# CIN tower of a DLRM: embedding columns by way of a DRAM scratch, and a tile's last partial sums on VectorE

## What is computed

```python
B, F0, D = (256, 39, 16)      # F0 = 39 fields, D = 16; the batch here is 1024
x0 = inputs; xk = inputs; outs = []
for W in filters:             # f0 (39*39, 128), f1 (128*39, 128), f2 (128*39, 128)
    b, f, d = x0.shape
    g = xk.shape[1]
    z = jnp.einsum('bfd,bgd->bfgd', x0, xk).reshape(b, f * g, d)
    cur = jnp.einsum('bpd,pm->bmd', z, W)
    outs.append(cur)
    xk = cur
result = jnp.sum(jnp.concatenate(outs, axis=1), axis=-1)
...
e = jnp.stack([tbl_0[ids[:, 0]], ..., tbl_38[ids[:, 38]]], axis=1)
```

## Time and profile before

| | |
|---|---|
| median of 3 runs | 1393.21 us (1392.9 to 1393.88) |
| profiled execution | 1393.13 us, of which the span of the instructions 1391.3 us |
| mean granted clock of TensorE | 0.998 |
| busy: TensorE, its weight loads | 93%, 70% |
| busy: VectorE, ScalarE, GpSimd | 70%, 55%, 75% |
| VectorE's MACs (L805) | 2944, 811.6 us |
| ScalarE's scaling (L667) | 2048, 585.8 us |
| GpSimd's adds (L364, L368) | 565.0 and 58.8 us |
| gathers (L341) | 312, 298.9 us |
| DMA | 72.97 MB, mean 52 GB/s |

### The profile page before, as it was taken

The page is one execution under the profiler, slowest core; times in us unless marked ns, Lnnn a source line. Parts: engine busy times, 40 slices in busy tenths (PEclk is TensorE's granted clock), DMA queues, the critical chain, the costliest instruction groups (busy, mean ns, idle before and its releaser), DMA issues.

```text
span 1391.3 us, 25265 instructions
## 1 busy us (share of the span) xinstructions
PE 1294.6 (93%) x5629; PEld 971.1 (70%) x5629; DVE 978.5 (70%) x3241; ACT 760.4 (55%) x2434; POOL 1038.3 (75%) x921
## 2 busy tenths in 40 slices
PE   0179999998999999999999999999999999999999
PEld 0057777776778777877778767877778777877754
DVE  2068778687876878688876778687885878688720
ACT  2136565466655566466664566466664565566631
POOL 7648868788787878788787878878787876566530
PEclk9999999999999999999999999999999999999999
DMA  8131122011211112111211112111211111111000
GB/s 220 25 112 53 47 70 64 6 54 46 80 53 52 47 38 74 27 53 47 79 53 52 47 24 64 50 53 47 78 53 53 46 25 58 51 52 45 1 1 0
DMA packets 73417, 72.97 MB, mean 52 GB/s; under 512 B 32428, under 2 KB 44690, under 8 KB 72716
## 3 DMA queue, kind: packets, MB, share of 16 engines
q1 hardware_dynamic: 60600, 67.88, 16.5%
q0 software_dynamic: 9984, 2.58, 2.2%
q10 hardware_dynamic: 2720, 1.48, 0.4%
HBM read 10.15 MB, written 0.00 MB: 7 GB/s over the span
## 4 chain that ended last, share of the span: by engine, by line
PE 50%; POOL 14%; DVE 11%; issue 10%; DMA 6%; ACT 5%; SPq 3%; DVEq 1%; POOLq 0%; ACTq 0%
PE ps L469 10%; PE ps L473 10%; PE ps L470 10%; PE ps L448 9%; DVE terms L805 9%; POOL terms L364 6%; POOL x_in L341 5%; PE ps L493 5%; DMA x_cols<-x_cols 4%; ACT terms L667 3%; DVE prods L777 3%; PE ps L558 2%; PE ps L483 2%; POOL prods_low L218 2%; DMA x_first<-x_cols 1%
## 5 line engine op out<-in xcount | busy, mean ns | idle before, releaser
L805 DVE SCALAR_TENSOR_TENSOR terms<-ps,x_scal,terms 128x128 f32<-128x128 f32 x2944 | 811.6, 346 | 276.0 <-PE ps L473 149.3
L667 ACT ACTIVATE terms<-ps,x_scal 128x128 f32<-128x128 f32 x2048 | 585.8, 375 | 388.6 <-PE ps L473 342.1
L364 POOL TENSOR_TENSOR terms<-terms 128x1024 f32<-128x1024 f32 (+2 forms) x384 | 565.0, 1471 | 168.2 <-DVE terms L805 142.9
L469 PE MATMUL ps<-w_high,x_high 128*128 128x512 f32 (+1 forms) x1280 | 592.5, 463 | 24.3 <-DVE terms L805 18.6
L473 PE MATMUL ps<-w_high,x_low 128*128 128x512 f32 (+1 forms) x1280 | 499.7, 390 | 6.1 <-ACT x_cols L619 5.6
L470 PE MATMUL ps<-w_low,x_high 128*128 128x512 f32 (+1 forms) x1280 | 497.8, 389 | 0.0
L341 POOL DMA_INDIRECT x_in<-in_tbl,ids_now x312 | 298.9, 958 | 100.5 <-issue 84.6
L469 PEld LDWEIGHTS ps<-w_high,x_high 128*128 128x128 f32 x1280 | 241.4, 189 | 136.5 <-DVE terms L805 50.5
L470 PEld LDWEIGHTS ps<-w_low,x_high 128*128 128x128 f32 x1280 | 242.4, 189 | 71.0 <-issue 29.8
L473 PEld LDWEIGHTS ps<-w_high,x_low 128*128 128x128 f32 x1280 | 241.2, 188 | 60.2 <-ACT x_cols L619 8.2
L448 PE MATMUL ps<-prods,w 117*128 117x512 f32 x262 | 135.3, 601 | 8.6 <-DVE prods L777 8.6
(11 more groups left out here) (45 smaller groups left out, 455.0 us busy)
## 6 DMA issues: line engine op xcount, KB each, us to landing
prods<-x_cols SPq DMA_DIRECT2D x192, 234.0 KB
x_first<-x_cols SPq DMA_DIRECT2D x96, 78.0 KB
x_in<-in_tbl,ids_now POOLq DMA_INDIRECT x312
x_cols<-x_cols SPq DMA_DIRECT2D x14, 312.0 KB
x_diag<-x_scal SPq DMA_DIRECT2D x256, 9.8 KB, 1.9
s<-in_f SPq DMA_DIRECT2D x3, 832.0 KB, 13.2
wt<-in_W_top ACTq DMA_DIRECT2D x1, 768.0 KB, 8.0
wt<-in_W_top ACTq DMA_DIRECT2D x1, 512.0 KB, 9.3
```

What stands on the lines that cost most here:

```text
L364: nc.gpsimd.tensor_tensor(t[:, 0:n], t[:, 0:n], t[:, n:2 * n], ALU.add).then_inc(s_tree, 1)
L469: nc.tensor.matmul(y, x1_high[:, par, at:at + P], high, start=True, stop=False)
L667: op = nc.scalar.activation(terms[:, u % 2, FB * ACT_BANKS.index(q) + i, :], ps[:, (BANKS * u + q) % RING, i * G:(i + 1) * G], ACT.Copy, s ...
L805: nc.vector.scalar_tensor_tensor(out=acc, in0=y, scalar=x0, in1=acc, op0=ALU.mult, op1=ALU.add).then_inc(s_mac, 1)
```

## The change

x0 is fetched by groups of 32 samples and no longer by batches. On the host, the 39 tables are joined into one, and the ids are ordered so that one indirect DMA fetches four fields of 32 samples; GpSimd adds the tables' first rows to the ids (`number_rows`). Ten gathers make a group. A DMA (`put`) writes the group to a scratch in DRAM, `rows`, and four DMAs (`load_cols`) read it back into x0_cols with the fields on partitions, the repeats included. The transposes, `store_cols` and `repeat` go. Gathers run three groups ahead (`AHEAD`). SP's queue is ordered anew (`feed`); w2 and the MLP's weights are loaded later, behind the first x_diag, from SP's queue, and TensorE waits for w2 after the second tile. GpSimd's tree ends at four slices (`TREE = (8, 4)`), and VectorE sums these four into x2 (`reduce`), for tile u - 1 behind bank 9 of tile u, ahead of a product that stands there. The diff, cut to its core:

```diff
-GATHERED, SUMMED = 8, 10
-TURNS = ((9, 7), (10, 0), (10, 4), (10, 8))
-TREE = (8, 4, 2)
+SAMPLES = P // GROUPS
+FOUR = P // SAMPLES
+FETCHES = -(-F // FOUR)
+AHEAD = 3
+TREE = (8, 4)
+LEFT = TREE[-1]
+REDUCE_AT = 9
...
+        def put(queue, bt, j):
+
+            queue.wait_ge(s_gather[j % 2], (bt * (GROUPS // 2) + j // 2 + 1) * (16 * FETCHES))
+            queue.dma_start(rows[j % GROUPS].rearrange("(n p) d -> p n d", p=P), x0_in[:, j % 2, :, :]).then_inc(s_put, 16)
+
+        def load_cols(queue, gf, j):
+
+            g = j % GROUPS
+            queue.wait_ge(s_put, gf * 16 + 16)
+            source = rows[g].rearrange("(f b) d -> f (b d)", b=SAMPLES)
+            for i in range(SPT + 1):
+                n = min(F, CYCLIC - i * F)
+                queue.dma_start(x0_cols[i * F:i * F + n, g * GCOLS:(g + 1) * GCOLS], source[0:n, :]).then_inc(s_load, 16)
...
+            def next_cols(gf, j):
+
+                sp.wait_ge(s_load, gf * (16 * (SPT + 1)) + 16 * (SPT + 1))
+                move_first(j)
+
+            def feed(bt, j, more=True):
+
+                gf = bt * GROUPS + j
+                move(gf, j)
+                if more:
+                    put(sp, bt, j + 1)
+                move_diag(gf, j)
+                if more:
+                    load_cols(sp, gf + 1, j + 1)
+                    next_cols(gf + 1, j + 1)
 
             load_ids(1)
-            sp.wait_ge(s_cols, 1)
-            repeat(slice(0, GCOLS), 1)
+            put(sp, 0, 0)
+            load_cols(sp, 0, 0)
+            next_cols(0, 0)
             move(0, 0)
+            next_cols(1, 1)
+            move(1, 1)
             sp.wait_ge(s_ones, 1)
             sp.wait_ge(s_scal, 1)
             for b in range(TB):
...
+            load_late()
+            put(sp, 0, 2)
+            move_diag(1, 1)
+            load_cols(sp, 2, 2)
+            next_cols(2, 2)
+            for j in range(2, GROUPS + 1):
+                feed(0, j)
+            with sp.Fori(1, NBATCH - 1) as bt:
+                load_ids(bt + 1)
+                for j in range(1, GROUPS + 1):
+                    feed(bt, j)
...
                     nc.gpsimd.tensor_tensor(t[:, 0:n], t[:, 0:n], t[:, n:2 * n], ALU.add).then_inc(s_tree, 1)
-                pool.wait_ge(s_tree, bt * (STEPS * len(TREE)) + len(TREE) * (u + 1))
-
-                pool.wait_ge(s_s3, bt * STEPS + u - 1 + CREDIT_S3)
-                nc.gpsimd.tensor_tensor(x2[:, u % 2], t[:, 0], t[:, 1], ALU.add).then_inc(s_x2, 1)
...
+            with pool.Fori(0, NBATCH - 1) as bt:
+                for u in range(STEPS):
+                    if u == TILES:
+                        pool.wait_ge(s_ids, bt * 16 + 3 * 16)
+                        pool.wait_ge(s_gather[1], (bt * (GROUPS // 2) + GROUPS // 2) * (16 * FETCHES))
+                        number_rows()
+                        pool.wait_ge(s_row, bt + 2)
+                    if u % TILES == 0:
+                        pool.wait_ge(s_put, (bt * GROUPS + u // TILES + AHEAD - 1) * 16)
+                    add_up(bt, u)
+                    for n in gathers(u):
+                        gather(u // TILES + AHEAD, n)
...
-                if turn_next:
-                    may_turn(bt, TURNS.index((u, q)))
+                if scalars_next:
+                    pe.wait_ge(s_load, (bt * GROUPS + u // TILES + 2) * (16 * (SPT + 1)))
...
+                    if u == 1 and q == BANKS - 1:
+                        pe.wait_ge(s_w2, 16)
...
-                store_first_cols(slice(0, GCOLS // D), 1)
                 store_scalars(0, 0, False)
-                store_first_cols(slice(GCOLS // D, BATCH), 3)
                 store_first(0, 0, FIRST_BANK)
+                act.wait_ge(s_put, 16)
+                act.wait_ge(s_load, 16 * (SPT + 1))
+                put(act, 0, 1)
+                load_cols(act, 1, 1)
                 store_x1(0, 0)
...
+            def reduce(bt, u):
+
+                dve.wait_ge(s_tree, bt * (STEPS * len(TREE)) + len(TREE) * (u + 1))
+                dve.wait_ge(s_s3, bt * STEPS + u - 1 + CREDIT_S3)
+                nc.vector.tensor_reduce(x2[:, u % 2], terms[:, u % 2, 0:LEFT, :].rearrange("p t g -> p g t"),
+                                        AX_X, ALU.add).then_inc(s_x2, 1)
...
                     if q in DVE_BANKS:
                         mac(bt, u, q)
+                    if q == REDUCE_AT and u > 0:
+                        reduce(bt, u - 1)
                     if front and (tile, q) in PRODUCTS:
                         multiply(bt, j, PRODUCTS.index((tile, q)), X1_BANK)
```

More of the change, by code:

```diff
@@ L161, in cin_tower @@
         s_top = sem("mlp_weights_loaded")
-        s_gather = sem("rows_gathered")
+        s_dense = sem("dense_loaded")
+        s_gather = [sem(f"rows_gathered{i}") for i in range(2)]
         s_ones = sem("x0_diag_cleared")
@@ L311, in _ @@
             for b in range(TB):
[L312 to L328, removed]
+                rows_b = slice(b * D, (b + 1) * D)
+                sp.dma_start(x0_diag[rows_b, 0, :, b, 0:F], x0_scal[rows_b, 0, :, :]).then_inc(s_diag[0], 16)
+            load_late()
[9 more added lines that the diff above has]
+                    feed(bt, j)
+            for j in range(1, GROUPS):
+                feed(NBATCH - 1, j, j < GROUPS - 1)
             for h in range(2):
@@ L401, in _ @@
+            for u in range(STEPS):
+                if u == 0:
+                    pool.wait_ge(s_put, (NBATCH * GROUPS - 2) * 16)
+                add_up(NBATCH - 1, u, u < STEPS - TILES)
+                if u < TILES:
+                    for n in gathers(u):
+                        gather(u // TILES + AHEAD, n)
         @block.tensor
@@ L507, in prologue @@
                 pe.wait_ge(s_dene, NBATCH // 4)
-                pe.wait_ge(s_gather, 16 * F)
-                for r in range(4):
-                    turn(r, r)
-                pe.wait_ge(s_cols, 1)
+                pe.wait_ge(s_load, 16 * (SPT + 1))
                 turn_scalars(0, 0)
@@ L527, in step @@
                 for q in range(BANKS):
-                    turns = not last and (u, q) in TURNS
+                    scalars = front and (tile, q) == SCALARS
                     if (tile, q) == SCALARS and j == 2:
                         pe.wait_ge(s_r, bt * 2 + CREDIT_R)
-                    cin2(bt, u, q, turns)
+                    cin2(bt, u, q, scalars)
                     if q == S3_AT and u >= 2:
                         sum_s3(bt, u)
-                    if turns:
-                        turn(TURNS.index((u, q)), MISC_BANK)
-                    if front and (tile, q) == SCALARS:
+                    if scalars:
                         turn_scalars(gf, j)
@@ L722, in step @@
                         store_s3(bt, u)
-                    if not last and (u, q) in TURNS:
-                        store_cols(bt + 1, TURNS.index((u, q)))
                     if front and (tile, q) == SCALARS:
@@ L844, in step @@
                         split_x1(gf, j)
[L846 removed]
+            prologue_then_batches(dve, step, prologue, lambda bt: reduce(bt, STEPS - 1))
 TOP = ("W_top1", "b_top1", "W_top2", "b_top2", "W_top3")
@@ L878 @@
     out = nc.dram_tensor("out_y", (B, 1), F32, kind="ExternalOutput").ap()
-    cin_tower(nc, ap["dense_ctx"], ap["ids"], [ap[f"tbl_{f}"] for f in range(F)],
+    rows = nc.dram_tensor("x0_rows", (GROUPS, FETCHES * P, D), F32, kind="Internal").ap()
+    cin_tower(nc, ap["dense_ctx"], ap["ids"], ap["first_row"], ap["tables"],
               *[ap[name] for name in TOP], ap["w0_pair"], ap["w0_mirror"], ap["f1"], ap["f2"],
-              ap["c_mask"], ap["c_eye"], out)
+              ap["c_mask"], ap["c_eye"], rows, out)
     r = run_bass_kernel_spmd(nc, [arrays], core_ids=[0])
```

154 lines of the change are left out of this document (55 added, 99 removed).

## The result

The changed kernel takes 1451.72 us, the median of four runs (1449.72 to 1452.47), against 1393.06 for the kernel before beside it (1392.34 to 1393.88). The ratio is 1.0419, with a 95% interval of 1.0401 to 1.0437. So it is slower, as forecast, but by 58.7 us and not by 22, and 3.7 us above the top of the range. The profiled execution has a span of 1449.9.

A forecast was written before the change was run, and what follows sets the result against it. TensorE was busy 1294.6 of 1391.3 us, gated by x2 through ScalarE's scale and VectorE's first MAC. 1391.3 - 37.6 - 25.9 - 6.9 + 89.4 + 0.5 + 1.9 + 3.0 - 2.2 = 1413.5, predicted 1415; range 1372 to 1448.

The forecast's parts named there:

- The length of the reduction: VectorE's sum of four slices into x2 takes 0.65 to 0.68 us, bounds 0.5 and 1.36.
- The turns of the two engines: ScalarE and VectorE alternate once per tile around the reduction: +2.98 us a group, +89.4 us over thirty groups.
- Rival (B): The strided reduction on VectorE takes twice as long: +59 us, 1474; 10%, in full or in part.
- Rival (A): ScalarE's and VectorE's turns hide behind TensorE's larger lead, leaving only gains: 1320, 10%; half the cost, 1367, another 10%.
- The start: Before the first tile, ten gathers, put and load_cols: first tile at 42.5 us, range 41 to 48, -37.6 us.
- The turn of a batch: Sixteen transposes, ScalarE's four stores and TensorE's waits for them go, seven times 3.7 us: -25.9 us.
- The two late x2: Two longer batches lose their excess from x2 ended late by GpSimd: -6.9 us.
- The feed: SP's queue gets one put and four loads per group; costed at nothing, with 12 us of slack per group.
- (C): Rival: put or loads end later than x_first is read; 1477 with 2 us over; 4%.
- w2: First batch: w2's late load stalls TensorE 4 us plus a 2.4 slow stretch, 6.5 instead of 8.7: -2.2 us.
- The end: Last group's VectorE pace +1.9 us; TensorE's wait for reduce(14) before the last layers +3.0 us.

The follow-up runs named there:

- neighbours: Changed kernel with the reduction reading 128 groups of four neighbouring values instead of four slices 512 bytes apart: 1417.2 us, ratio 1.0171.
- The earlier reduction: Changed kernel with REDUCE_AT 6 instead of 9, so VectorE sums three banks earlier: 1358.04 us, ratio 0.9744.
- the idle one: Changed kernel with x2 from a VectorE add of two slices behind bank 6, and an unread strided reduction behind bank 9: 1373.0 us, 0.9858.
- the last version: Changed kernel with x2 by a VectorE add behind bank 6, w2's wait in cin3, row numbering after GpSimd's two split_low: 1326.83 us, 0.9519.
- every second value: Changed kernel with the reduction reading 128 groups of four values, each 8 bytes behind the last: 1418.29 us, ratio 1.018.
- the eight steps: Changed kernel plus eight VectorE reductions at its end of an unused still buffer, summands 4 to 512 bytes apart: 1450.88 us in one run.
- the moved wait: Changed kernel with TensorE's wait for w2 moved from the end of the second tile to ahead of cin3: 1447.38 us, ratio 1.0392.

## Why the prediction was right in its mechanism and wrong in its size

Put against the sum, by stretches between first matmuls of a batch (the forecast's column is its terms laid on the earlier trace rows; the last batch is what the sum leaves):

| us | forecast | changed kernel | neighbours |
|---|---|---|---|
| first tile starts | 42.5 | 42.5 | 42.6 |
| batch 0 | 160.3 | 167.6 | 163.8 |
| batches 1 to 6, each | 165.1 | 168.9 | 164.8 |
| batch 7 and the end | 220 | 226.6 | 220.4 |
| span | 1413.5 | 1449.9 | 1415.5 |

- **The length of the reduction** is the term that was mis-sized, and the step of the prediction that failed. It took L785's 0.68 us as the nearest row, for its 512 elements, and it named the difference, 512 bytes between summands, without giving it weight. It is 1.07. The prediction's own slope, 2 us per group for each us, makes 0.8 us of these 0.39, and 0.98 was measured (40.07 against 39.09), which is 2.5 for each us. Thirty groups are 29 us, the first group and the end the rest of the 34.5. The slope of 2 also doesn't fit the +59 that the prediction gives for twice as long: 0.68 x 2 x 30 is 41.
- **The turns of the two engines** were right in kind and in size. The neighbours' run has the forecast's 0.68 and gives 39.09 for 39.12, and 1417 for 1415. The earlier reduction and the idle one show that most of it is the wait and not the work: 2.4 us of a group against 1.4. ScalarE's own wait was sized too low, though. It is 345.9 us, and with neighbours still 292.9 in 118 tiles, three times the 100 forecast. That cost TensorE nothing more, as T2 and T3, which have about half of it, are as long as before. The 123 waits of VectorE for ScalarE were as said.
- **Rival (B)**, a dearer strided reduction, was the one that came, to a little over half of its "twice as long". It got 10% with "against: nothing" beside it. A rival with nothing against it should have had more, and the range, which left out most of it, should have reached at least to 1474.
- **Rival (A)**, turns that hide, is refuted by the neighbours' run; its 1320 is near what the last version reaches, where they do hide.
- **The start** was right to 0.1 us (42.48), and that is in part luck. The tenth gather started at 17.29 for 15.8, x0's columns were there 3.1 us after the store for 5.2, and from there it took 16.7 us for 15.5. What is left is just the 1.0 that was put on top of the sum of 41.5. Eight other kernels with all but the same instructions up to there start their first tile between 42.3 and 45.6. The store to DRAM, which had no row, landed 2.4 us after its issue began; the SBUF copy behind the 2.0 of the sum landed 2.0 after its own began (62.64 to 64.63), so the store is 0.4 dearer, and the 0.6 for issuing was counted on top. The section of the Trainium skill that the prediction names here, DMA: Bandwidth & Descriptors, "Anatomy of one DMA", describes DMAs that GpSimd issues, while this store goes out from SP's queue; no run tells what part of the 0.4 us the receipt has.
- **The turn of a batch** was taken as worth 3.7. A batch of the last version is 153.9 (656.19 to 810.09), against 156.9 for an undisturbed one before, although its four groups are 0.1 to 0.3 slower each: that makes the turn worth 3.6. With neighbours, too, a batch has the forecast's length. Only if one starts from the reduction and adds the new path, the turn is 2.3, since the two costs overlap. The two late x2 have gone, as forecast: batches 1 to 6 are all between 168.8 and 169.0.
- **The feed** cost nothing, and (C) didn't come: no wait of TensorE for columns stands in the steady groups.
- **w2** was forecast with a stall of 4 and a slow stretch of 2.4. The prediction's own numbers, 10 + 12.5 us to the landing against 17 to the wait, give 5.5 and not 4, and batch 0 before was 8.5 over (156.74 against 148.2) and not 8.7. The stall was 7.16, the slow stretch 2.7 (T2 at 13.27 for 10.59), as the load was issued 3.3 us later than the ten after the start that were assumed. With neighbours batch 0 stays 3.5 over the forecast, and 2.9 of these are the stall, which is 6.9 in that run; the rest lies in the turns of the first group, which were too cheap with +0.5.
- **The end** was +1.9 and +3.0. Measured are 2.5 for the three short tiles of the last group (8.04, 8.21, 8.21 for 7.33) and 7.1 from the start of the last tile on (74.5 for 67.4). With neighbours these are 1.3 and 4.8, so three quarters of that miss are again the length of the reduction.

## What to carry to other kernels

Work given to an engine with idle time is cheap only where nobody waits for it: here the kernel with 137 us of reductions behind the last bank is 125 us slower than the last version, and the one with the same 137 us three banks earlier 31, so its place should be chosen by who needs the result, not by the share of busy time. When the nearest row for a new operation differs in its access pattern, the pattern is the unknown: the range must hold the dearer price, and a few idle instructions at the end of a kernel measure it. A tree of adds can leave two contiguous halves, whose add costs VectorE a third of a strided sum of four (0.32 against 1.07 us).

## What the runs showed of the hardware

- A VectorE `tensor_reduce` of 128 x 512 fp32 from SBUF takes 0.68 us with 4 or 8 bytes between the values of a sum, and 1.00 to 1.07 with 16 to 512 bytes (the neighbours, every second value, the eight steps, the changed kernel).
- A 2.56 MB load issued by SP held up an 80 KB store that ScalarE issued 3.6 us later, from 2.4 to 11.8 us until its successor could be issued; the store's end came 0.4 us behind the load's.
- The 1280 pieces of 64 bytes that go to DRAM in one DMA landed 2.4 us after its issue began in 28 of 32 cases. One issued at 66.50, while w2 and the MLP's weights were coming in, took 6.3.
- The first tile took 11.9 to 12.9 us in three kernels (the eight steps, the moved wait, the last version) and 8.5 to 9.5 in the eight others with the new path of x0, though the tile's instructions are the same in the eight steps' kernel and the changed one. This is open.
